# Matmuls with zero weights beside the scans of a Mamba-style image network

## The reference, cut to what matters

```
xi, z = split(x @ in_proj_w.T)
xc = silu(depthwise_conv3x3(xi) + conv_b)
xs = four orders of xc                      # k = 0..3
dts, Bs, Cs = split(x_proj_w[k] @ xs)
delta = softplus(dt_w @ dts + dt_b);  A = -exp(A_logs)
h = exp(delta * A) * h + (delta * u) * B_t  # one step of the scan
y_t = sum over the 16 states of h * C_t
y = layernorm(y1 + y2 + y3 + y4 + Ds * xs) * silu(z)
out = y @ out_proj_w.T
```

## Time and profile before

| | |
|---|---|
| median of 3 runs | 11572.21 us (11567.04 to 11578.72) |
| profiled execution, its own time | 11564.55 us |
| its span in the profile | 11562.8 us |
| busy: PE, DVE, ACT, POOL | 8819.7, 10132.7, 7059.3, 9737.8 us |
| mean granted TensorE clock | 0.741 of 2.4 GHz |

### The profile page before, as it was taken

How to read it: one execution, slowest core, us unless ns; L and a number is a source line. 1 busy time by engine, 2 the same in 40 slices (tenths; PEclk the granted TensorE clock), 3 DMA queues, 4 the chain that set the end, 5 groups by cost and what they waited for, 6 DMA issues and landing times.

```text
span 11562.8 us, 94504 instructions
## 1 busy us (share of the span) xinstructions
PE 8819.7 (76%) x26272; PEld 2210.7 (19%) x26272; DVE 10132.7 (88%) x6006; ACT 7059.3 (61%) x10794; POOL 9737.8 (84%) x4231
## 2 busy tenths in 40 slices
PE   6876678876879677769777787787787977777756
PEld 2211111211112111212112121122111221121212
DVE  3899998999889998989989999899989999898871
ACT  4665555665556555667555765566655666567646
POOL 3899988899888998989988888888888889898850
PEclk8875577875779667769777787788677976777766
DMA  3666689566775556656766668957677656565540
GB/s 100 143 139 132 142 150 162 143 138 142 159 160 144 139 145 156 153 130 147 166 150 152 133 141 171 157 133 154 130 159 161 144 133 159 151 149 126 130 118 6
DMA packets 1781802, 1631.74 MB, mean 141 GB/s; under 512 B 1323982, under 2 KB 1325296, under 8 KB 1781276
## 3 DMA queue, kind: packets, MB, share of 16 engines
q1 hardware_dynamic: 1781276, 1625.69, 63.7%
HBM read 625.58 MB, written 194.51 MB: 71 GB/s over the span
## 4 chain that ended last, share of the span: by engine, by line
DVE 16%; PE 16%; issue 15%; POOL 12%; ACT 7%; DMA 3%; SPq 3%; DVEq 0%; POOLq 0%; ACTq 0%
POOL pr L1632 8%; DVE hs L1553 7%; DVE ps L1538 6%; DVE hs L1549 3%; PE ps L1032 3%; PE ps L861 2%; PE ps L1019 2%; PE ps L826 1%; PE ps L1010 1%; ACT dec L1288 1%; POOL bup L1646 1%; POOL dur L1646 1%; PE ps L994 1%; POOL us L1623 1%; SPq L720 1%
## 5 line engine op out<-in xcount | busy, mean ns | idle before, releaser
L1632 POOL TENSOR_TENSOR pr<-hs,crep 128x1024 f32<-128x1024 f32 x3072 | 7183.5, 2354 | 1194.5 <-PE ps L1032 571.8
L1553 DVE TENSOR_TENSOR_SCAN hs<-dec,carry,ps 128x1024 f32<-128x1024 f32 x1728 | 4054.7, 2346 | 240.4 <-POOL pr L1632 14.0
L1538 DVE TENSOR_TENSOR ps<-ps,dur 128x1024 f32<-128x1024 f32 x2304 | 2790.1, 1211 | 513.9 <-PE ps L1019 372.5
L1019 PE MATMUL ps<-sbc,selb 96*128 96x512 bf16 x4608 | 1844.5, 493 | 1789.8 <-DVE hs L1553 1248.3
L1288 ACT ACTIVATE dec<-dtr,ac 128x1024 f32<-128x1024 f32 x2304 | 2610.9, 1136 | 436.4 <-DVE hs L1553 427.7
L1032 PE MATMUL ps<-pr,red 128*32 128x512 f32 x12288 | 2285.0, 827 | 33.0 <-POOL pr L1632 24.5
L1295 ACT ACTIVATE carry<-hs 128x1 f32<-128x1 f32 x2304 | 456.9, 199 | 2434.7 <-DVE hs L1553 2265.4
L1553 DVE TENSOR_TENSOR_SCAN hs<-dec,zero,ps 128x1024 f32<-128x1024 f32 x576 | 1351.5, 2346 | 86.0 <-ACT dec L1288 14.1
L826 PE MATMUL ps<-xb,tapw 96*96 96x512 f32 x2304 | 1187.2, 637 | 55.9 <-ACT sd L1122 53.4
L1019 PEld LDWEIGHTS ps<-sbc,selb 96*128 96x128 bf16 x4608 | 382.5, 108 | 3922.6 <-DVE hs L1553 2313.5
L1288 ACT ACTIVATE ps<-dtr,ac 128x1024 f32<-128x1024 f32 x768 | 848.4, 1105 | 400.0 <-DVE hs L1553 399.8
(11 more groups left out here) (224 smaller groups left out, 7595.9 us busy)
## 6 DMA issues: line engine op xcount, KB each, us to landing
dtr<-de SPq DMA_DIRECT2D x768, 512.0 KB, 8.0
dur<-us SPq DMA_DIRECT2D x768, 512.0 KB, 8.6
crep<-bc_d SPq DMA_DIRECT2D x512, 512.0 KB, 6.6
ust<-u_d SPq DMA_DIRECT2D x256, 384.0 KB, 5.9
y_d<-yst SPq DMA_DIRECT2D x768, 128.0 KB, 3.3
sd<-y_d SPq DMA_DIRECT2D x448, 192.0 KB, 5.1
brep<-bc_d SPq DMA_DIRECT2D x128, 512.0 KB, 5.6
u_d<-sd SPq DMA_DIRECT2D x64, 384.0 KB, 3.2
```

What stands on the lines that cost most here:

```text
L1019: mm = pe.matmul(ps[:, SLOT + 2 * (n % RS) + hf, :], selb[:, i % GT // 2, :], sbc[:, w % 2, B * hf:B * (hf + 1)], start=True, stop=True)
L1538: dve.tensor_tensor(slot(n), slot(n), dur[:, 2 * (G % 2) + i % 2, :], ALU.mult).then_inc(bu_v, 1)
L1553: dve.tensor_tensor_scan(hs[:, n % RH, :], dec[:, others(n) % RD, :], slot(n), init, ALU.mult, ALU.add).then_inc(scan_v, 1)
L1632: pool.tensor_tensor(pr[:, n % RP, :], hs[:, n % RH, :], crep[:, q, :], ALU.mult).then_inc(prod_g, 1)
```

## The change

A tile `nil` of zeros is set once on POOL. At the end of the ticks of six of eight tiles (`open_sum` is false for the tiles 2 and 3 of a group, between the last `reduce2` of a sum and the first of the next) TensorE does three matmuls with the weights `nil` that add zeros to `YB`. In the tiles 2 and 3 it does the next tile's `fill` twice instead, the second time over the first. The added matmuls have no waits of their own.

```diff
+BUSY = 3
...
+        nil = sb("nil", [CH, 128], BF16)
...
+            def open_sum(i):
+                return i % GT not in (2, 3)
+
+            def keep_busy():
+                for _ in range(BUSY):
+                    pe.matmul(ps[:, YB, :], nil[:, :], selb[:, :, :].rearrange("p q n -> p (q n)"),
+                              start=False, stop=False, skip_group_check=True)
...
             def fill(n):
                 ...
-                for hf in range(2):
-                    mm = pe.matmul(ps[:, SLOT + 2 * (n % RS) + hf, :], selb[:, i % GT // 2, :],
-                                   sbc[:, w % 2, B * hf:B * (hf + 1)], start=True, stop=True)
+                for again in range(1 if open_sum(i - 1) else 2):
+                    for hf in range(2):
+                        mm = pe.matmul(ps[:, SLOT + 2 * (n % RS) + hf, :], selb[:, i % GT // 2, :],
+                                       sbc[:, w % 2, B * hf:B * (hf + 1)], start=True, stop=True)
                 mm.then_inc(fill_p, 1)
...
                         next(side, None)
+                    if n >= 4 and open_sum(i):
+                        keep_busy()
...
             pool.memset(eps[:, :], 1e-5)
+            pool.memset(nil[:, :], 0.0)
             pool.memset(zero[:, :], 0.0).then_inc(set_g, 1)
```

## The result

The changed kernel takes 11802.85 us (median of 4 runs, 11796.78 to 11818.48) against 11574.33 us for the one before on the same chip: ratio 1.0201, 95% interval 1.0186 to 1.0217. The prediction was 11,707 us, slower, in a range up to 11,960. So the sign and the range held. The forecast had been 135 us more than before; 228 us more came.

What follows compares the result with a forecast made beforehand. VectorE's chain of products and scans was taken as the bound, with TensorE nearly full beside the convolution. 11564.6 + 195 (convolution) - 60 (side stretches) + 0 (rest) gave 11,700, comparable 11,707 us; range 11,450 to 11,960.

Steps and rivals of the forecast that it cites:

- The price of a call: Three filler matmuls on TensorE: 0.65 us, 0.74 us if the weight change shows, about 1.4 us at the low clock.
- the pair at 5468.20: Two fill matmuls in the profile before, ending 0.52 us after their start instead of 0.43, put down to changing weights.
- Convolution stretches: The 7.5 stretches with convolution work, TensorE nearly full: likely plus 195 us, 26 us each, bounds 70 and 300 us.
- the 9 to 25 us that the work alone gave: Forecast growth of each convolution stretch even if TensorE never idles.
- the 12 us of idle time: TensorE idle time assumed to remain per convolution stretch, making its growth about 21 to 37 us.
- Side stretches: Stretches with post and attention work: likely minus 60 us, from a gain of 200 to a loss of 150 us.
- backlog: Side stretches: late fills from queued TensorE work, about 120 of 290 us of waits, of which 90 would go.
- the filler delays late fills: Rival: in side stretches filler costs 1.4 us before 150 fills, on top of convolution's 200; about 11,940 us, chance 0.18.
- The rest, 0: Scan-only stretches, memset, head and tail: no change, DVE's chain covering the additions; scan-only bounds 0 and 70 us.
- The clock pays: Rival: side stretches gain 230 us, more than the convolution's loss of 110; about 11,450 us, chance 0.22.
- The change doesn't do what it says: Rival: zero-weight matmuls don't hold the clock, side stretches stay at 0.73, scan-only at 0.57; over 12,050 us, chance 0.06.

Runs made afterwards that it cites:

- tiles 5 and 6 alone: Changed kernel with filler only in tiles 5 and 6 of each group of eight, no repeated fills; 11638.75 us, ratio 1.0045 to the kernel before.
- short filler: Changed kernel with filler matmuls of 128 instead of 512 columns; 11642.46 us, ratio 1.0051 to the kernel before.
- four calls and repeats: Changed kernel without filler in tiles 5 and 6 of a group, four calls instead of six; 11740.4 us, ratio 1.0136 to the kernel before.

## Why the prediction was right in sign and short in size

**The price of a call** was right. In the changed trace, with one late `fill` (PE and DVE, start and us):

```profile
6171.25 3.73 PE L863 MATMUL ps<-sd,eye 96*96 96x512 f32 x4 [3.31 <-DMA sd<-y_d]
6174.77 1.49 PE L999 MATMUL ps<-selb,nil 96*128 96x512 bf16 x3
6176.19 2.02 PE L1024 MATMUL ps<-xdf,tapw 6*96 6x512 f32 x2
6178.13 3.73 PE L863 MATMUL ps<-sd,dg 96*96 96x512 f32 x4
6181.65 1.49 PE L999 MATMUL ps<-selb,nil 96*128 96x512 bf16 x3
6183.07 1.94 PE L1047 MATMUL ps<-pr,red 128*32 128x512 f32 x8
6184.94 0.82 PE L999 MATMUL ps<-selb,nil 96*128 96x512 bf16 x3
6185.60 0.59 PE L1034 MATMUL ps<-sbc,selb 96*128 96x512 bf16 x2
...
6186.30 1.23 DVE L1555 TENSOR_TENSOR ps<-ps,dur 128x1024 f32<-128x1024 f32 x1 [8.34 <-PE ps L1034]
```

From start to start a call takes 1.42 us at the low clock and 0.66 us at the full one, as forecast. That the pair at 5468.20 was slower because the weights change isn't shown: behind the faster pair at 5466.05 they change too.

**Convolution stretches: mechanism right, size 122 us instead of 195.** TensorE does become the bound there. The seven full stretches grew by 14 to 21 us, inside the 9 to 25 us that the work alone gave. The mis-sized term is the 12 us of idle time that I let stay. With a full TensorE only 2 to 4 us of it are left: ACT's eviction, which had held TensorE for 9.2 us at 5202, holds it for 1.4 us. The first 20 us or so of added work per stretch, about what TensorE had idled, were nearly free. The added work is an estimate from the calls' measured lengths: 13 us (tiles 5 and 6 alone: 20 calls of 0.65) changed the convolution steps by +3 us, and some 19 to 21 us (short filler, 60 calls of 0.17 to 0.21, and 8.6 of repeats) by +18 us, 2 per stretch; 35 us (four calls and repeats) by +71, or 9 per stretch; 47 us by +122, or 16; and 86 us by +338, or 45.

**Side stretches: wrong sign, plus 70 us instead of minus 60.** The step that failed is that backlog would mostly vanish at the full clock, and the wait for `fill` outside the convolution with it. It rose instead, from some 300 to 404 us. I compared a late `fill` at the old clock with the same one at the full clock. But the clock rose only from 0.75 to 0.86 beside `post`, and it stayed lower just where the `fill` was late: over the time that DVE waited for `fill` its mean was 0.78 beside `post` and 0.63 beside attention, in steps whose mean is 0.86. The chain above shows one such place. The same scan in the kernel before reads:

```profile
6042.78 3.73 PE L861 MATMUL ps<-sd,eye 96*96 96x512 f32 x4 [2.08 <-DMA sd<-y_d]
6046.44 2.02 PE L1010 MATMUL ps<-xdf,tapw 6*96 6x512 f32 x2
6048.39 3.73 PE L861 MATMUL ps<-sd,dg 96*96 96x512 f32 x4
6052.05 1.94 PE L1032 MATMUL ps<-pr,red 128*32 128x512 f32 x8
6053.92 1.03 PE L1019 MATMUL ps<-sbc,selb 96*128 96x512 bf16 x2
...
6055.06 1.23 DVE L1538 TENSOR_TENSOR ps<-ps,dur 128x1024 f32<-128x1024 f32 x1 [5.63 <-PE ps L1019]
```

TensorE waits for a load in both. Its clock is at the low level from that wait on in both, nearly to the end of the chain. Two windows of the changed trace show it, just before the chain and along it (columns as above):

```profile
6150.00:6167.00 17.00, 14.80 (x61) 4.91 (x63) 16.47 (x11) 8.16 (x15) 15.73 (x8) 1.00 1.15 157
6168.00:6185.00 17.00, 13.75 (x25) 3.48 (x26) 9.83 (x5) 7.18 (x11) 7.67 (x4) 0.50 0.38 117
```

The two calls of filler that now stand between the matmuls run at the low clock. From the first L861 to the `fill` it was 11.14 us and is 14.35 us; DVE waits 8.34 instead of 5.63 us. This is the rival "the filler delays late fills", at less than half of its size. The run without additions beside `post` gave 0.55% back, some 64 us, so that they cost is shown. That all of it is filler in front of late fills is argued from this place and not shown: short filler came out nearly as dear there, the other order within the tile took only 5 us off these steps, and without any additions they were 16 and 29 us longer in two profiles.

**The rest, 0: plus 27 us in scan-only steps.** The cover by DVE's own chain isn't complete: over the 25 steps the wait for `fill` rose from 15 to 37 us. The tail behind the last scan has no additions. It was 11 us longer in this profile and 3 to 13 us longer in all the others, at a slightly lower clock (0.66 to 0.69 for 0.70). Why the kernel before had the shorter tail in its one profile stays open.

**Luck in the sum.** The convolution was put 73 us too high, the side stretches 130 us too low, and the rest and the tail 38 us too low. That the time came out within 96 us of the forecast is in part these errors cancelling.

**Rivals.** "The clock pays" failed most clearly with six matmuls a call: clock 0.91, ratio 1.0513. "The change doesn't do what it says" failed on the clock: in the scan-only steps it is 0.61 with the repeats alone and 0.75 with the filler as well. The rule of the Trainium skill ("TensorE: Matmul & The Clock Gate", What's actually happening), that the clock follows how busy the array has been, agrees with that: zero weights count as work.

## What to carry to other kernels

Before adding work to an engine to keep its clock up, find the stretches in which that engine is already nearly full. There the clock has little to give, and added work is paid for once it exceeds the idle time that was left: some 20 us a stretch here. An engine that works in order can't do filler during a wait. The filler then stands in front of the work that is already late, here at the low clock. The same filler cost less ahead of the side work than behind it (1.0136 for 1.0201), but most of that gain didn't come where it was expected. The repeated fills, which fit the idle time, cost nothing and raised the clock, and in this kernel the higher clock brought nothing either.

## What the runs showed of the hardware

Matmuls with all-zero weights raise the granted clock: in the scan-only steps it was 0.57 before, 0.61 with the repeated fills alone, and 0.75 with three filler matmuls a call as well. A low clock isn't evidence of lost time: with the repeated fills alone the mean clock rose from 0.741 to 0.768 and the time didn't change (ratio 1.0000). Beside a full TensorE most of the wait for ACT's evictions went, which had looked like idle time that would remain (9.2 to 1.4 us at 5202 and 5309, 3.3 to 1.7 us in the first full stretch). VectorE's product read from PSUM took 1215 to 1218 ns in the convolution stretches with the additions instead of 1211 or 1212.
